# Gated attention and low-rank block on one core: the last quarter of tile 7's product four moved ahead of product one of tile 8

## The reference

```python
def fake_quant(x, scale, zp):
    q = jnp.clip(jnp.round(x / scale + zp), 0.0, 255.0)
    return (q - zp) * scale

x = x + tanh(g_xattn) * (fake_quant(layernorm(x)) @ fake_quant(ctx_4096))   # ctx: 2 x 2048 x 2048
weight = (U * S[None, :]) @ V.T                                             # rank 512
x = x + tanh(g_ffn) * (layernorm(x) @ weight.T)                             # in the kernel: (x @ V) @ (U*S).T
```

## Time and profile before

| | |
|---|---|
| time, median of 3 runs | 588.7 us (588.44 to 588.7) |
| time of the profiled execution | 588.18 us |
| its span in the trace | 586.4 us |
| granted TensorE clock | 1.0 |
| TensorE busy | 568.3 us (97%) |
| DVE busy | 447.8 us (76%) |
| ACT busy | 236.0 us (40%) |
| GpSimd busy | 196.3 us (33%) |
| bytes moved | 102.73 MB, mean 175 GB/s |

### The profile page before, as it was taken

The page is one execution under the profiler, slowest core; times in us unless marked ns, Lnnn a source line. Parts: engine busy times, 40 slices in busy tenths (PEclk is TensorE's granted clock), DMA queues, the critical chain, the costliest instruction groups (busy, mean ns, idle before and its releaser), DMA issues.

```text
span 586.4 us, 7496 instructions
## 1 busy us (share of the span) xinstructions
PE 568.3 (97%) x2688; PEld 259.5 (44%) x2688; DVE 447.8 (76%) x797; ACT 236.0 (40%) x268; POOL 196.3 (33%) x146
## 2 busy tenths in 40 slices
PE   1899999999999999999999999999999999999998
PEld 0344444444444444444444444444444444444444
DVE  6959999997178982679978799798597986888222
ACT  4799888822123423648713612102530135103200
POOL 2989850000406127847541720220044005310000
PEclk9999999999999999999999999999999999999999
DMA  8999995638927796789975262423854086403722
GB/s 275 387 386 387 337 268 130 127 102 172 272 66 216 175 247 188 210 232 386 268 166 156 57 138 57 125 74 64 224 108 135 9 176 165 125 1 69 165 55 107
DMA packets 145941, 102.73 MB, mean 175 GB/s; under 512 B 108785, under 2 KB 109041, under 8 KB 145905
## 3 DMA queue, kind: packets, MB, share of 16 engines
q1 hardware_dynamic: 136912, 84.96, 55.0%
q10 hardware_dynamic: 8992, 17.30, 9.0%
HBM read 58.99 MB, written 16.78 MB: 129 GB/s over the span
## 4 chain that ended last, share of the span: by engine, by line
PE 94%; DMA 2%; POOL 1%; SPq 1%; issue 1%; DVE 0%; DVEq 0%
PE bank L616 23%; PE bank L692 19%; PE bank L661 12%; PE bank L697 9%; PE bank L755 9%; PE bank L760 9%; PE bank L756 9%; PE bank L579 2%; DMA v_hl<-in_ctx_dram 2%; SPq L331 1%; POOL u8r L270 1%; POOL q L279 1%; PE bank L711 0%; PE bank L592 0%; SPq L341 0%
## 5 line engine op out<-in xcount | busy, mean ns | idle before, releaser
L285 POOL TENSOR_SCALAR ring<-ring,bvec 128x2048 f32<-128x2048 f32 x16 | 33.4, 2089 | 259.2 <-DVE bvec L1245 259.2
L616 PE MATMUL bank<-q,qT 128*128 128x512 f16 x512 | 117.8, 381 | 0.0
L692 PE MATMUL bank<-v_hl,xT 128*128 128x512 f16 x448 | 101.3, 379 | 0.0
L290 POOL TENSOR_TENSOR ring<-ring,corr 128x512 f32<-128x512 f32 x64 | 88.9, 1419 | 22.6 <-ACT corr L967 21.6
L755 PE MATMUL bank<-u_hl,hbuf 128*128 128x512 f16 x208 | 78.9, 379 | 0.0
L756 PE MATMUL bank<-u_hl,hbuf 128*128 128x512 f16 x208 | 78.8, 379 | 0.0
L279 POOL TENSOR_SCALAR q<-u8r,const 128x1024 f16<-128x1024 uint8 x52 | 66.8, 1295 | 33.6 <-ACT u8r L864 29.8
L616 PEld LDWEIGHTS bank<-q,qT 128*128 128x128 f16 x512 | 50.3, 98 | 61.4 <-issue 1.7
L692 PEld LDWEIGHTS bank<-v_hl,xT 128*128 128x128 f16 x448 | 43.8, 98 | 52.2
L915 ACT ACTIVATE ln<-ln,const 128x1 f32<-128x1 f32 x16 | 4.7, 295 | 144.0 <-DVE ln L1342 144.0
L1416 DVE SCALAR_TENSOR_TENSOR ring<-bank,cy,ring 128x512 f32<-128x512 f32 x63 | 46.2, 745 | 17.4 <-PE bank L760 17.3
(11 more groups left out here) (173 smaller groups left out, 782.4 us busy)
## 6 DMA issues: line engine op xcount, KB each, us to landing
out_dram<-ring SPq DMA_DIRECT2D x63, 256.0 KB, 3.4
ring<-in_x_dram SPq DMA_DIRECT2D x62, 256.0 KB, 4.3
v_hl<-in_ctx_dram SPq DMA_DIRECT2D x26, 512.0 KB, 11.5
stage<-in_ctx_dram ACTq DMA_DIRECT2D x17, 512.0 KB, 5.9
u_hl<-in_L_ffn_V_dram SPq DMA_DIRECT2D x8, 512.0 KB, 11.4
corr<-in_ctx_dram ACTq DMA_DIRECT2D x8, 512.0 KB, 6.7
stage<-in_ctx_dram SPq DMA_DIRECT2D x6, 512.0 KB, 11.4
q<-in_ctx_dram ACTq DMA_DIRECT2D x4, 512.0 KB, 9.9
```

The lines of the kernel that those rows point to most:

```text
L290: nc.gpsimd.tensor_tensor(xq(t, n), xq(t, n), corr[:, n * W:(n + 1) * W], ALU.add).then_inc(x1_pre, 1)
L616: mm = nc.tensor.matmul(unit_bank(t, n)[:, :], qT_of(t)[:, k, :], q2[:, n, k, :], start=(k == 0), stop=(k == KT - 1))
L692: nc.tensor.matmul(h_bank(u)[:, :], x_home(u, g)[:, half, k % 8, :], v_hl[:, k, 0, :], start=(g == 0 and a == 0 and half == 0), stop=False)
```

## The change

The last quarter of product four of tile 7 (12 matmuls) stood behind product one of tile 9 and ahead of product three of tile 8. It now follows the other three quarters, ahead of product one of tile 8. Its sum on DVE, its store and the load that takes its place in `ring` move forward too. No instruction is added, removed or altered.

```diff
@@ sync
             load_x(11, 1)
             load_x(11, 2)
+            store(7, 3)
+            load_x(11, 3)
             q_transpose(10)
             x_transpose(8)
-            store(7, 3)
             x_transpose(9)
-            load_x(11, 3)
             h_transpose(8)
@@ tensor
             colsum_of_sums(2)
-            mm4(7, 0, 3)
+            mm4(7)
             s1_part(8, 0)
             s1_part(8, 1)
             colsum_of_sums(3)
             s1_part(8, 2)
             s1_part(8, 3)
             s1(9)
-            mm4(7, 3)
             mm3(8)
             mm3(9)
             mm4(8)
@@ vector
             y_unit(7, 2)
             row_correction(9)
+            y_unit(7, 3)
             x1_unit(8, 0)
...
             x1_unit(9, 3)
             stats2(9)
-            y_unit(7, 3)
             x_lo(9)
             t2_and_t3(0)
             hid_lo(8)
```

## The result

| | before | changed |
|---|---|---|
| median (13 runs each) | 588.57 us | 589.7 us |
| span of the profiled execution | 586.4 us | 587.4 us |
| TensorE busy | 568.3 us | 569.1 us |
| ratio of the times | | 1.0019, 95% interval 1.001 to 1.0027 |

The change costs 1.1 us by the medians and 0.6 to 1.6 by the interval. It lies clear of zero and, at 0.19%, just under the 0.2% line that I had set between "the same" and "slower".

The account below looks back on a forecast made before the run. The kernel was taken as a TensorE-bound queue of matmuls with hardly a hole. Terms 0 + 0 + 1.36 + 0 gave +1.4 us, 588.7 + 1.4 = 590.1 us (0.24%), range 589.7 to 590.4.

Parts of the forecast that it names:

- What the change does to TensorE itself: 0.: TensorE around tiles 8 and 9: the same 12 matmuls run 2.59 us at another place, adding no wait; 0.
- TensorE may wait 0.1 to 0.35 us: At product three of tile 9: its transpose may land late; 0.1 to 0.35 us, not added to the sum.
- 2.49 later, not 1.93.: DVE's subtraction at 345.85: starts 2.49 us later, since the freed 0.66 stood in a gap spent waiting for ACT.
- The pause absorbs 1.04.: DVE's pause before tile 8's hidden, awaiting ACT's copy: absorbs 1.04 us, so the shift falls from 2.49 to 1.45.
- is not slack: DVE's wait for ACT's hidden copy of tile 9: the same chain through ACT, so it moves by 1.45 us too.
- unseen slack: Stretch 355 to 377 through ACT: 1.36 us or more hides the loss, 588.7; part of a rival with chance 0.22.
- 0.09 us of slack: Before the first pair's third product: 0.14 - 0.05 = 0.09 us free, so it starts 1.45 - 0.09 = 1.36 later.
- Is it given back later?: Later pairs of products: the loss is neither recovered nor increased; 0, with bounds -0.4 and +0.3 us.
- Rival C: Two DVE additions beside GpSimd: their order turns round and the hole closes; 589.7, chance 0.10, within the forecast's own 0.68.
- the one wait that DVE's product sums still cause is 0.39: TensorE's waits in the kernel before: DVE's product sums hold it just once, for 0.39 us.
- The store and the load: SP's queue around the transposes of tiles 8 to 10: moving both earlier costs 0 and gains 0.
- The signs: Changed trace: product three of tile 8 within 0.1 of 343.58, no DVE pause, third product held 1 us or more.

Follow-up runs that it names:

- e5: Changed kernel with the second half of the prepared sums on DVE moved later, behind the first quad's differences; ratio 0.9993 to the kernel before.
- e6: Kernel before with the second half of the prepared sums on DVE moved later, behind the first quad's differences; ratio 0.9984 to the kernel before.
- e1: Kernel before with the quarter moved on TensorE alone; its sum, store and load stay at the old places; ratio 1.002 to the kernel before.
- e3: Kernel before with two more statistics instructions on DVE directly behind the low half of tile 8's hidden, behind the pause; ratio 1.0025 to the kernel before.
- e4: Kernel before with two more statistics instructions on DVE directly ahead of the low half of tile 8's hidden, in the pause; ratio 1.0006 to the kernel before.
- e2: Changed kernel with the quarter's store and the load back at their old places in SP's list; ratio 1.0019 to the kernel before.
- e7: Changed kernel with the first pair's first sum on DVE ahead of two sums of tile 8's product four; ratio 1.0018 to the kernel before.
- e8: Kernel before with two quarters of tile 7's product four, not one, behind product one of tile 9; ratio 1.0001 to the kernel before.
- e9: Changed kernel with two more statistics instructions in DVE's idle time ahead of product one's last quarter of tile 8; ratio 1.0032 to the kernel before.

## Why the prediction was right

- **"What the change does to TensorE itself: 0."** Right. Product three of tile 8 follows product one with no wait, and the 12 matmuls cost 2.59 us at either place. The first transpose of tile 8 was in time, as reckoned.
- **"TensorE may wait 0.1 to 0.35 us" at product three of tile 9.** Right: 0.25, not in the sum because the longer wait swallows it, which e5 against e6 shows (0.26).
- **"2.49 later, not 1.93."** Right in kind: 2.55. Of DVE's freed 0.66, 0.62 turned into idle time behind ACT, and e1 priced the slot at 0.04. I had allowed 0.10 for it.
- **"The pause absorbs 1.04."** Right in kind; it took 2.55 - 1.42 = 1.13. The 0.09 more is that an instruction of DVE behind another starts some 0.08 before the recorded end of the first, so the idle time of a bracket is a little less than what a pause can take. e3 and e4 agree: the two instructions cost 1.18 behind the pause and 0.05 ahead of it, so the pause took 1.13.
- **The chain through ACT and back "is not slack" and "moves by 1.45 too".** Right: 1.41 at the quantising of tile 11, 1.40 at the first sum. The chance that I gave to unseen slack there was not needed; e3 excludes it.
- **"0.09 us of slack" ahead of the third product.** Wrong: there was none. I took the start of the pair from the chain and not from the timeline, and read the third product as standing directly behind the second. In the timeline the first starts at 374.66, the third 3.62 later, and 16 matmuls take 3.45 (e6). So it was already held 0.17 by the same sum, with no wait listed, since the recorded spans of matmuls (0.38, starts 0.216 apart) overlap and hide a gap of that size. The third product follows its sum by 0.14 in both kernels; the 0.05 that I used is from the seventh, where it is 0.05 in both, and why the two differ isn't shown. That the step did no harm is luck: the slack that wasn't there (0.09) and the length by which the pause was taken too short (0.09) cancel. 2.49 - 1.04 - 0.09 = 1.36 was forecast; 2.55 - 1.13 = 1.42 came on DVE, and 1.41 at the third product.
- **"Is it given back later?" 0, between -0.4 and +0.3.** Right: the hole at the seventh product is listed as 0.39 in both kernels. Rival C did not happen, as GpSimd and DVE moved together. The bound of -0.4 was too narrow, though, and "the one wait that DVE's product sums still cause is 0.39" was wrong: the list of waits and the 0.48 idle of the earlier trace rows leave out what overlapping spans hide. In the kernel before DVE held TensorE for 0.17, 0.55 and 0.25 us in this pair, 0.97 in all, and e6 gained 0.98.
- **The store and the load: 0.** Right (e2).
- **The signs.** The absolute places that I gave for the changed trace all came 0.39 to 0.45 earlier than said, product three of tile 8 at 343.19 instead of within 0.1 of 343.58, because of the varying start. Against product three of tile 8 they hold to 0.1: no wait there, DVE's pause gone, the quantising of tile 11 and the first sum later as reckoned, and TensorE held 1.17 before the third product.
- **The size.** Forecast +1.4, in the trace +1.4, by the medians +1.1 with 0.6 to 1.6. The two agree within the interval. That the trace and the medians differ by 0.3 isn't explained; e1 and e2 with the same distances have medians of +1.33 and +1.31. With 0.67 on slower by over 0.2%, I put more on one side of that line than a forecast of 0.24% carries.

The loss is thus a change of cover. The quarter gave TensorE 2.59 us of work while DVE finished the second layer norm of tile 9. Without it DVE came 2.55 late, 1.13 went into a pause, and the remaining 1.42 went through DVE, ACT and DVE again to a sum that TensorE already waited for. That it is TensorE's order and not DVE's or SP's is shown by e1 and e2, the pause by e3 and e4, the length of the chain by e5 and e6, and the last sum by e7. The link through ACT's queue has no experiment of its own: it is read from the rows (quantising ahead of the hidden copy), e3's delay passed through it nearly whole, and in e5 and e6 DVE no longer waits for ACT there.

## What to carry to other kernels

When an independent piece of matmuls is moved within a full queue, ask what was using the time that it gave, and follow that chain past the next stage: the price here fell due some 37 us behind the quarter's old place, at a product of another stage. Each pause in the chain is worth its length once; a pause that another engine ends is worth something only if that engine isn't fed by the chain itself. And work of the late engine that isn't needed at once belongs in a pause whose end the chain itself sets: that gave 1.0 us here (e6), where placing the matmuls better gave nothing (e8).

## What the hardware showed unexpectedly

- Two more instructions on DVE cost 0.35 us at a place 45 to 70 us later, in three kernels (e3, e4, e9), always at the same sum of the second quad, which started 2.35 us after its product's first matmul instead of 2.00. In the eight other traces it starts at 2.00, and there DVE has 556 instructions ahead of it, in these three 558. e9 speaks against the timing as the cause, as the two were absorbed there. That it goes by the number of instructions ahead fits all eleven traces but isn't shown: one or three more were not tried. The instruction queue q14 has a transfer 1.1 us behind the start of that sum in the kernel before and the changed one, and 0.7 to 1.0 us behind it in the three with the loss; whether the fetch of instructions is the cause wasn't tried and stays open.
- The first matmul of product three of tile 8 stands at 343.19 to 344.04 in the eleven traces, though TensorE has the same matmuls ahead of it in all, in another order in some. The spread arises in the first 55 us. From there on the eleven run alike to 0.01 us up to the change, but for e1 and e5, which lose another 0.35 and 0.44 at 153.6 us, where product one waits for a transpose. A span is therefore a poor measure of a difference under 1 us in this kernel, and a distance within the trace a good one: it repeated to 0.04 us in the changed kernel, e1, e2 and e9.
